# Integer feed-forward of a four-layer network on one core: rounding and norm by ScalarE, fp32 rows turned while still shifted, weights made integers in the attention before it

## The reference, cut to what matters

```python
def _weight_quant(w):
    scale = 1.0 / jnp.clip(jnp.mean(jnp.abs(w)), 1e-05)
    return jnp.clip(jnp.round(w * scale), -1.0, 1.0) / scale
def _act_quant(x):
    scale = 127.0 / jnp.clip(jnp.max(jnp.abs(x), axis=-1, keepdims=True), 1e-05)
    return jnp.clip(jnp.round(x * scale), -128.0, 127.0) / scale
def _bitlinear(x, w):
    return jnp.einsum('bsi,oi->bso', _act_quant(x), _weight_quant(w))
gate = jax.nn.silu(_bitlinear(x, w_gate))      # 256 -> 1024
up = _bitlinear(x, w_up)                       # 256 -> 1024
return _bitlinear(gate * up, w_down)           # 1024 -> 256
...
x = x + _L1_ffn_ref(_layernorm(x, axis=-1), L1_ffn_w_gate, L1_ffn_w_up, L1_ffn_w_down)
```

## Time and profile before

| | |
|---|---|
| median of 3 runs | 3504.17 us (3503.16 to 3506.55) |
| the profiled execution | 3504.71 us, its span 3503.0 us |
| busy over the whole span | PE 90%, PEld 68%, DVE 70%, ACT 31%, POOL 27% |
| the integer feed-forward | from about 1214 to 1481.6 us of the span |
| of it, constants and weights | up to 1235.9 us |
| of it, first to last tile | 1242.6 to 1481.6 us |
| granted TensorE clock over the span | 0.948 of full |

### The profile page before, as it was taken

The page is one execution under the profiler, slowest core; times in us unless marked ns, Lnnn a source line. Parts: engine busy times, 40 slices in busy tenths (PEclk is TensorE's granted clock), DMA queues, the critical chain, the costliest instruction groups (busy, mean ns, idle before and its releaser), DMA issues. The chain is left out here.

```text
span 3503.0 us, 67687 instructions
## 1 busy us (share of the span) xinstructions
PE 3144.3 (90%) x27654; PEld 2380.6 (68%) x27670; DVE 2451.7 (70%) x6457; ACT 1078.8 (31%) x1919; POOL 940.4 (27%) x1000
## 2 busy tenths in 40 slices
PE   5998999897699756577799999999999997999999
PEld 4776766565477623366688888888888885777444
DVE  5787355001577799844688888888888884778666
ACT  3444211221344344444322222222222212444000
POOL 2332000232243200000144434434435343333000
PEclk9999999999799977788799999999999997999999
DMA  3100210343300000021200000000000002010000
GB/s 124 38 26 16 81 50 13 88 115 77 111 26 26 11 1 1 22 68 38 97 1 1 1 1 1 1 1 1 2 1 1 2 1 75 26 38 2 13 19 18
DMA packets 81171, 108.26 MB, mean 31 GB/s; under 512 B 11744, under 2 KB 62176, under 8 KB 80480
## 3 DMA queue, kind: packets, MB, share of 16 engines
q1 hardware_dynamic: 74720, 95.40, 8.3%
q0 software_dynamic: 6144, 8.52, 1.3%
HBM read 87.00 MB, written 16.91 MB: 30 GB/s over the span
## 5 line engine op out<-in xcount | busy, mean ns | idle before, releaser
L2035 POOL TENSOR_TENSOR pk_hisig<-pk_hihot,pk_sigs 128x512 f16<-128x512 f16 x512 | 520.6, 1044 | 668.3 <-DVE pk_hihot L2242 667.4
L2096 PE MATMUL pk_ps<-pk_nt,ew_downT 128*128 128x128 f32 x4096 | 515.5, 279 | 0.0
L2096 PEld LDWEIGHTS pk_ps<-pk_nt,ew_downT 128*128 128x128 f32 x4096 | 479.7, 192 | 15.3 <-issue 15.3
L2137 PE MATMUL pk_ps<-ew_up,pk_act_h 128*128 128x256 f32 x2048 | 450.4, 381 | 0.9 <-DVE pk_act_h L2230 0.9
L2137 PEld LDWEIGHTS pk_ps<-ew_up,pk_act_h 128*128 128x128 f32 x2048 | 388.8, 191 | 53.1 <-issue 1.0
L2043 ACT ACTIVATE pk_act_h<-pk_ps 128x512 f32<-128x512 f32 x256 | 153.0, 597 | 542.3 <-PE pk_ps L2096 542.3
L2243 DVE TENSOR_TENSOR pk_lohot<-pk_iota_h,pk_ps 128x1024 f16<-128x1024 f16 x256 | 312.1, 1219 | 0.0
L568 DVE RECIPROCAL a_rden<-a_ps_o 128x256 f32<-128x256 f32 x96 | 168.4, 1754 | 159.9 <-PE a_ps_o L458 159.9
L557 DVE TENSOR_REDUCE a_mx<-a_ps_s 128x8 f32<-128x1024 f32 x192 | 226.1, 1219 | 54.4 <-PE a_ps_s L432 54.3
L273 ACT ACTIVATE a_pT<-a_ps_t 128x512 f32<-128x512 f32 x384 | 209.0, 599 | 145.8 <-PE a_ps_t L441 145.6
L2416 PE MATMUL mo_ps<-mw_we,mo_xnT 128*128 128x512 f32 x512 | 225.6, 599 | 0.0
(11 more groups left out here) (353 smaller groups left out, 5433.5 us busy)
## 6 DMA issues: line engine op xcount, KB each, us to landing
ro_w<-in_L_W SPq DMA_DIRECT2D x16, 1024.0 KB, 7.1
a_ctx_t<-in_ctxT SPq DMA_DIRECT2D x24, 512.0 KB, 3.8
a_tau<-in_tau SPq DMA_DIRECT2D x24, 256.0 KB, 4.1
a_delta<-in_delta SPq DMA_DIRECT2D x24, 256.0 KB, 4.3
X<-in_x SPq DMA_DIRECT2D x4, 1024.0 KB, 9.5
row_dram<-sh_row SPq DMA_DIRECT2D x8, 512.0 KB, 3.2
sum_dram<-sh_new SPq DMA_DIRECT2D x8, 512.0 KB, 2.9
X<-sum_dram SPq DMA_DIRECT2D x4, 1024.0 KB, 9.6
```

The costliest lines, as they stand in the source:

```text
L2035: ins = pool.tensor_tensor(hisig[:, buf, n, :, :, :], hi, sig2.broadcast_to([P, TP, 2, ECH]), ALU.mult)
L2096: ins = pe.matmul(hid.bank(f"h{c}")[:, j * P:(j + 1) * P], downT[:, k, e * P:(e + 1) * P], nt[:, s, k, :], start=(k == 0), stop=(k == KC - 1))
L2137: ins = pe.matmul(tail.bank("y")[:, 0:D], act_h[:, s, c, :], up[:, c, :], start=(c == 0), stop=(c == ECH - 1))
```

## The change

It has two parts.

The weights' integers are made in the second attention. A class `BitWeights` holds what that takes, and `attention` calls it where it is given as `integers`. ScalarE takes the magnitudes of one matrix (Abs over 128x2048 with an accumulated sum) at the end of tiles 20, 21 and 22. TensorE adds them over the partitions in tile 28, into three free columns of the bank of the output rows. VectorE makes the scales behind tile 28's statistics. GpSimd rounds one matrix in three passes behind `rows` in each of tiles 29, 30 and 31. Output rows of tile 27 wait for VectorE to have read the three sums.

In the feed-forward the norm of x goes to ScalarE (scale and bias per row). The rounding of x is one instruction on VectorE (scale, add ROUND) and that of h one on ScalarE (`h_rounded`). The clips are gone: the factor is made from the largest magnitude, so no value passes 127. What is transposed is the shifted fp32 row, and ROUND is subtracted as the columns are copied out of PSUM. The 1024 columns of h in fp32 fill two PSUM banks, so they are copied in two halves, and the down matmuls wait for each half by itself. `h` has two buffers, and the three scales are one instruction.

```diff
+    def magnitudes(self, act, n):
+        if n == 0:
+            self.w.wait(act)
+        else:
+            act.wait_ge(self.sums_ready, n)
+        act.activation(self.sized[:, :], self.raw[n][:, :], ACT.Abs,
+                       accum_out=self.asum[:, n:n + 1]).then_inc(self.sums_ready, 1)
+    def totals(self, pe, dst):
+        pe.wait_ge(self.consts, 2)
+        pe.wait_ge(self.sums_ready, 3)
+        pe.matmul(dst, self.ones[:, :], self.asum[:, :], start=True, stop=True,
+                  skip_group_check=True).then_inc(self.summed, 1)
+    def scales(self, dve, src):
+        dve.wait_ge(self.consts, 2)
+        dve.wait_ge(self.summed, 1)
+        dve.tensor_scalar(self.wmean[:, 0:3], src, 1.0 / (D * INNER), 1e-5, ALU.mult, ALU.max).then_inc(
+            self.mean_link, 1)
+        dve.wait_ge(self.mean_link, 1)
+        dve.reciprocal(self.wscale[:, :], self.wmean[:, 0:3]).then_inc(self.scales_ready, 1)
+    def rounded(self, pool, n):
+        r, at = self.raw[n][:, :], 3 * n
+        pool.wait_ge(self.scales_ready, 1)
+        pool.tensor_scalar(r, r, self.wscale[:, n:n + 1], ROUND, ALU.mult, ALU.add).then_inc(self.round_link, 1)
+        pool.wait_ge(self.round_link, at + 1)
+        pool.tensor_scalar(r, r, ROUND, 1.0, ALU.subtract, ALU.min).then_inc(self.round_link, 1)
+        pool.wait_ge(self.round_link, at + 2)
+        pool.tensor_scalar(self.wb[self.names[n]][:, :], r, -1.0, None, ALU.max).then_inc(self.round_link, 1)
...
# attention: ScalarE, GpSimd, TensorE (twice), VectorE
+                    if integers and g == GROUPS - 3 and u < 3:
+                        integers.magnitudes(act, u)
...
+                    if integers and not more and u > 0:
+                        integers.rounded(pool, u - 1)
...
+                        if integers and not more and u == 1:
+                            pe.wait_ge(integers.mean_link, 1)
                         output_rows(t - 2, u % 2)
...
+                    if integers and not more and u == 0:
+                        m_after_y(t)
+                        integers.totals(pe, ps_m[:, D:D + 3])
...
+                    if integers and is_last(g) and u == 0:
+                        integers.scales(dve, ps_m[:, D:D + 3])
...
# bit_ffn, ScalarE
-                act.wait_ge(h_ready, t + 1)
-                act.activation(hq[:, :], h[:, :], ACT.Identity, bias=neg_round[:, 0:1]).then_inc(hq_ready, 1)
-                ht.wait_full(act, t, "ht")
-                ht.take(act.activation(hqT[:, :, :], ht.bank("ht")[:, :].bitcast(BF16).rearrange(
-                    "p (k n) -> p k n", n=P), ACT.Copy), "ht")
+            def h_rounded(t):
+                act.wait_ge(asc_ready, t + 1)
+                act.activation(hr[:, :], h[:, t % 2, :], ACT.Identity, scale=asc[:, t % 2, 1:2],
+                               bias=shift[:, 0:1]).then_inc(hr_ready, 1)
+            def h_columns(t):
+                for n in range(2):
+                    ht.wait_full(act, t, f"ht{n}")
+                    ht.take(act.activation(hqT[:, 4 * n:4 * n + 4, :], ht.bank(f"ht{n}")[:, :].rearrange(
+                        "p (k n) -> p k n", k=4), ACT.Identity, bias=shift[:, 1:2]), f"ht{n}")
...
# bit_ffn, VectorE: gone are the three passes over each matrix, the norm, and of each tile
-            def scaled(v, s, a):
-                return dve.tensor_scalar(v, v, asc[:, s, a:a + 1], -128.0, ALU.mult, ALU.max)
-            def rounded(v):
-                return dve.tensor_scalar(v, v, 127.0, ROUND, ALU.min, ALU.add)
-            def x_integers():
-                return dve.tensor_scalar(xq[:, :], xn[:, :], ROUND, None, ALU.subtract)
+            def x_rounded(t):
+                dve.tensor_scalar(xn[:, t % 2, :], xn[:, t % 2, :], asc[:, t % 2, 0:1], ROUND, ALU.mult,
+                                  ALU.add).then_inc(xr_ready, 1)
```

## The result

| | before | after |
|---|---|---|
| median of 4 runs, us | 3505.02 (3503.16 to 3506.55) | 3457.45 (3454.2 to 3459.26) |
| ratio, 95% interval | 1 | 0.9865 (0.9852 to 0.9877) |
| profiled execution: span, time, us | 3503.0, 3504.7 | 3457.5, 3459.26 |
| mean granted clock | 0.948 | 0.959 |

The kernel became faster by 1.35%, 47.6 us. The forecast was 3434 us in a range of 3425 to 3456: the sign was right, the size was 23 us off, and the measured time lies 1.5 us above the range.

The account below looks back on a forecast made before the run. VectorE was taken to set the feed-forward's pace, TensorE to bound the second attention. Terms -19.8 - 50.8 - 2.7 + 1.0 + 2.4 = -69.9 us, off 3504.2, gave 3434 us; own range 3425 to 3443, with rivals 3425 to 3456 (0.85).

Parts of the forecast that it names:

- the price of a pass on GpSimd: Second attention: nine weight passes over 2048 columns priced like casts, 1.87 us each, 1.95 with a wait.
- the forecast's own term: End of the second attention: GpSimd's nine passes and four tiles' additions make its last addition end later, +2.4 us.
- GpSimd is slow: Rival, weight passes in the attention: each takes twice the cast's time, 18.5 us more, 3453 us; chance 0.15.
- The clock: Rival, feed-forward tiles: transposes do not keep the clock up, a tile takes about 6.4 us, 3456 us; chance 0.15.
- The tile period: Feed-forward's 31 tile periods: each falls from 7.34 to 5.7 us, -50.8 us.
- the ring: Feed-forward tile: rounding of h, transposes, copies, output sums, gate matmuls and silu wait in turn through three engines, 5.77 us.
- One sign: Expected in the profile of the feed-forward's tiles: VectorE idle about 0.8 us a tile and waiting for silu.
- the set-up: Front of the feed-forward: the weights' sums and rounding leave it, first h at 1222.8 in place of 1242.6, -19.8 us.
- the end: Feed-forward's end, from the last tile's h to the end of its statistics: 8.8 in place of 11.5 us, -2.7 us.
- the magnitudes: Second attention: ScalarE's first magnitude pass delays the copy of output rows and TensorE's next projection piece, +1.0 us.
- the waits of TensorE and VectorE in the last group: Attention from tile 27: output rows wait for VectorE's read of the sums; between 0 and 1.2 us, not added.

Follow-up runs that it names:

- turned order: Changed kernel with TensorE's gates of tile t+2 ahead of t's output sums, x transposes ahead of h's, ScalarE's x copy ahead of norm and h columns: 3430.22 us.

## Why the prediction was wrong, and where it was right

**The step that failed** is the price of a pass on GpSimd: "I take the casts, as the passes have one tensor in", 1.95 us for each of nine. That is right for the three mult-add passes (2.0), and wrong for the six others (7.1 and 5.4). Per matrix 14.5 in place of 5.85 us, three times: +25.9 of the 26.6 us by which the term was off. With all nine passes in forms that the casts' price fits, the forecast's own term came out at +3.1 and the time at 3431. The trace of before has no pass with two scalars on GpSimd, so the price was bounded, and the bound did not hold: 4 us a pass from above (two inputs, 2.5 ns a column) lies under both prices measured, 5.4 and 7.1 us.

**Of the rivals** the one called "GpSimd is slow" is what happened, at 4.8 us a pass in the mean in place of its 4.0. Its reason was not: it named the per-row factor and the two operations, and the pass that has both is the quickest of the three. The Trainium skill ("GPSIMD Engine Reference", section 3.1) puts up to two operations at one price; worked out from its figures, the estimate is 1.76 us a pass. Four pairs here come near it with 1.9; a single operation at 5.36 and the other pairs at 7.1 do not, and the measurement decides.

**The clock** did not fall. The granted clock over the 31 periods is 0.99, with TensorE busy for 127.3 / 172.4 = 74% of the time (forecast 75%), though in each tile it does only fp32 transposes, or waits, from the end of the up matmuls to the output sums (in the tile of the timeline above from about 1344.1 to 1346.85). By the rule of "TensorE: Matmul & The Clock Gate" (Part 4) in the Trainium skill, that transposes do not count as busy in the same way, this rival would have been the forecast; the trace speaks against it here. No run holds transposes alone, so how the chip counts them stays open.

**The tile period** was a term of the right mechanism and somewhat the wrong size: 5.563 us in place of 5.7, worth 4.3 us in 31 periods. By the ring's steps in the timeline after: rounding with hand-over 1.29 (forecast 1.38), transposes to the first copy 0.70 (0.64), the copies 1.27 (1.29), from these to the gate matmuls 0.50 (0.74), to silu 0.69 (0.54), to the next rounding 1.15 (1.18), together 5.60. The largest difference is between the copies and the gate matmuls, where the forecast has a hand-over of 0.14 and 0.60 for four output sums. That the ring, not an engine, sets the pace was tested: turned order, same work, 4.72 us. One sign was named wrongly: VectorE is idle for 0.89 us a tile (forecast 0.8), but what it waits for is ScalarE's norm of x, 0.7 us a tile, and not silu.

**The other terms** held: the set-up -19.76 (-19.8), the end -2.91 (-2.7), the magnitudes +0.81 (+1.0; one pass takes 1.91 us and its read-out 0.18), the waits of TensorE and VectorE in the last group within 0.5 (between 0 and 1.2). The tile loop and the set-up are independent: the loop alone gives 5.526 us a tile, the weights' move alone the same 19.6 and 29.0 us.

**Not of the change**: the stretch ahead of tile 20, to which the change adds only two small memsets on GpSimd at about 892 us, is 2.6 us longer in the trace after than before. Of this 1.6 us are there by 346 us, ahead of any added instruction. In the profiled runs of the ten kernels the stretch ends between 1114.0 and 1119.5 us, whatever was edited. It is 2.6 us of the difference of the spans, and I can't say what sets it.

## What to carry to other kernels

A price for GpSimd holds for one form of instruction, not for a kind: before work is moved there, each pass is to be measured with its exact operations and their order, and written as mult-add or min-max where it can be, even if one of the two operations does nothing (times 1.0). An engine with idle time on average can still be on the path if its queue also holds what the others wait for: here the slow passes hurt because the next tile's addition stood behind them, and the clip, given to ScalarE's idle time as a Sign, cost nothing. When a loop's period is longer than every engine's busy time in it, follow the ring of waits and change the order in which its links are issued; here that took 26 us off the loop with no work taken out.

## What the runs showed of the hardware that was not expected

- GpSimd, tensor_scalar over 128 x 2048 fp32: mult-add, add-mult, mult-mult, min-max 1.9 us; a single operation (mult, subtract, min, max) 5.36 to 5.44; subtract-add, subtract-min, add-add, add-min, mult-min, mult-subtract, max-min 7.1. A result in bf16 changes nothing (5.36 with and without), and a constant in place of a per-row factor saves 0.08 us at most (1.98 to 1.90, 5.44 to 5.37). Max-min takes 3.7 times as long as min-max. Add alone was not tried.
- These prices are the same to 0.1 us beside other engines' work as without it: from 1197.84 to 1210.40 us of the changed kernel, with VectorE busy for 9.4 and TensorE for 11.3 of 12.6 us, the two slow forms take 7.10 and 5.37, alone 7.08 and 5.36. VectorE's long instructions there read PSUM; no run has others beside a pass.
- ScalarE's Abs and Sign over 2048 columns take 1.91 and 1.99 us, and neither has a table load ahead of it among ScalarE's work of the attention.
